# Sobel, attention and feed-forward tower: the carried edge rows of gy are written before the root's argument instead of after it

## What is computed

```python
kx, ky = _sobel_kernels()          # sy = [[1,2,1],[0,0,0],[-1,-2,-1]]
Ix = _dwconv(x, kx)
Iy = _dwconv(x, ky)
G = jnp.hypot(Ix, Iy)
return jnp.sum(G, axis=1)
...
h = jnp.concatenate([cls_tok, h], axis=1)
h = h + attention(layernorm(h))
h = h + ffn(layernorm(h))
```

## Time and profile before

| | |
|---|---|
| median of 3 runs | 1623.98 us (1623.11 to 1624.61) |
| the profiled execution | 1622.37 us, span 1620.3 us |
| VectorE busy | 1373.8 us, 85% of the span |
| PE busy | 839.6 us, 52% |
| ScalarE busy | 699.8 us, 43% |
| GpSimd busy | 110.1 us, 7% |
| DMA, mean | 35 GB/s |

### The profile page before, as it was taken

The page is one execution under the profiler, slowest core; times in us unless marked ns, Lnnn a source line. Parts: engine busy times, 40 slices in busy tenths (PEclk is TensorE's granted clock), DMA queues, the critical chain, the costliest instruction groups (busy, mean ns, idle before and its releaser), DMA issues.

```text
span 1620.3 us, 12694 instructions
## 1 busy us (share of the span) xinstructions
PE 839.6 (52%) x3318; PEld 655.5 (40%) x3318; DVE 1373.8 (85%) x2145; ACT 699.8 (43%) x1250; POOL 110.1 (7%) x154
## 2 busy tenths in 40 slices
PE   6663200466447743456537754256626764388543
PEld 3332100355336532344426543145525643376433
DVE  1999998899879999899879999899888999722676
ACT  1312332364375544164356553245446653132562
POOL 0000000001101000002101100002010100000000
PEclk9777655766569876667568976577568886577776
DMA  7000500013303510104302610104120300100001
GB/s 192 1 13 14 111 0 0 1 20 52 62 10 59 112 39 1 29 1 71 59 13 41 129 39 1 28 1 72 32 40 10 62 12 28 27 1 0 1 0 27
DMA packets 33421, 57.15 MB, mean 35 GB/s; under 512 B 6410, under 2 KB 23354, under 8 KB 31674
## 3 DMA queue, kind: packets, MB, share of 16 engines
q0 software_dynamic: 21024, 29.11, 11.1%
q1 hardware_dynamic: 12026, 26.31, 7.1%
q10 hardware_dynamic: 288, 0.79, 0.2%
HBM read 22.84 MB, written 4.25 MB: 17 GB/s over the span
## 4 chain that ended last, share of the span: by engine, by line
DVE 30%; issue 26%; ACT 15%; PE 12%; DMA 1%; DVEq 0%; ACTq 0%; SPq 0%
DVE arena L531 9%; DVE arena L528 6%; PE psum L1722 2%; ACT arena L1273 2%; DVE arena L872 2%; PE psum L1672 2%; PE psum L1694 1%; PE psum L1723 1%; PE psum L1576 1%; DVE red L544 1%; PE psum L1758 1%; ACT arena L1409 1%; ACT arena L1169 1%; DVE others L531 1%; ACT zT L1418 1%
## 5 line engine op out<-in xcount | busy, mean ns | idle before, releaser
L528 DVE TENSOR_TENSOR arena<-arena 128x768 f32<-128x768 f32 (+2 forms) x534 | 486.7, 967 | 45.8 <-ACT arena L1207 23.1
L531 DVE SCALAR_TENSOR_TENSOR arena<-arena 128x768 f32<-128x768 f32 (+2 forms) x224 | 201.4, 948 | 0.1
L1590 PE MATMUL psum<-zT,w1q 128*128 128x257 f32 x512 | 150.1, 431 | 41.8 <-ACT wout L1303 25.2
L1590 PEld LDWEIGHTS psum<-zT,w1q 128*128 128x128 f32 x512 | 111.3, 220 | 68.1 <-issue 27.5
L1576 PE MATMUL psum<-gpad,win 128*128 128x257 f32 x288 | 86.0, 442 | 54.9 <-ACT gpad L1285 54.9
L1238 ACT ACTIVATE arena<-arena 128x768 f32<-128x768 int16 x32 | 27.0, 843 | 175.6 <-DVE arena L531 175.2
L1694 PE MATMUL psum<-arena 128*128 128x257 f32 x128 | 50.6, 563 | 86.5 <-ACT arena L1392 65.3
L1576 PEld LDWEIGHTS psum<-gpad,win 128*128 128x128 f32 x288 | 62.6, 223 | 71.9 <-ACT gpad L1285 61.0
L531 DVE SCALAR_TENSOR_TENSOR arena<-img 128x768 f32<-128x768 f32 x88 | 79.5, 949 | 7.0 <-issue 6.4
L504 POOL DMA_DIRECT2D h<-others x60 | 51.7, 862 | 416.6 <-DVE others L531 347.7
L1169 ACT ACTIVATE arena<-arena 128x256 f32<-128x256 f32 x65 | 23.3, 409 | 118.4 <-DVE arena L531 68.2
(11 more groups left out here) (222 smaller groups left out, 1993.5 us busy)
## 6 DMA issues: line engine op xcount, KB each, us to landing
img<-x SPq DMA_DIRECT2D x36, 258.0 KB, 7.0
h<-others POOLq DMA_DIRECT2D x60, 128.0 KB, 2.7
arena<-nrows_mem POOLq DMA_DIRECT2D x18, 384.0 KB, 4.4
arena<-arena POOLq DMA_DIRECT2D x18, 384.0 KB, 4.1
arena<-img POOLq DMA_DIRECT2D x18, 384.0 KB, 4.9
out<-out SPq DMA_DIRECT2D x16, 256.0 KB
img<-x SPq DMA_DIRECT2D x48, 64.5 KB, 7.7
win<-w_in SPq DMA_DIRECT2D x4, 768.0 KB, 5.4
```

Of the source, the lines that this page charges most:

```text
L528: return v.tensor_tensor(o, a, b, op)
L531: return v.scalar_tensor_tensor(out=o, in0=a, scalar=s, in1=b, op0=op0, op1=op1)
L1590: ins = mm((A0, A1, B0, B1)[i % 4][:, 0:S], w1q[:, k, t * P:(t + 1) * P], zT[:, k, b, :], start=(k == 0), stop=(k == DT - 1))
```

## The change

The two writes of the next pair's edge rows move on VectorE from slot 5 to slot 4, ahead of whatever stands there, and each gets a wait for `hisq`, since it overwrites the q that ScalarE squares. They are then issued ahead of the root's argument, and no longer between the argument and the root. On ScalarE the negated copies of these rows move from behind slot 6 to behind slot 5: ahead of the square of the f16 value (line 1249), and no longer ahead of the next one (line 1254). There are 9 pairs with the edge rows (pairs 0 to 2 of three groups) and 6 with the negated copies (pairs 0 and 1). No instruction of an engine is added.

```diff
@@ magnitude_rows, VectorE
                 def with_carry(k):
-                    if k == 5 and i < PAIRS - 1:
+                    if k == 4 and i < PAIRS - 1:
                         for f in F:
+                            dve.wait_ge(hisq, n2 + f + 1)
                             edge_row(tmp[f][1], 2 * i + f + 4).then_inc(carried, 1)
                     slot(k)
@@ magnitude_rows, ScalarE
                     if k == 3 and i < PAIRS - 1:
                         for f in F:
                             s.activation(nrows[:, f], img[:, :, 2 * i + f + 2, 2:2 + W], ACT.Copy, scale=-1.0).then_inc(neg_rows, 1)
-                    if k == 6 and i < PAIRS - 2:
+                    if k == 5 and i < PAIRS - 2:
                         for f in F:
                             act.wait_ge(carried, g * (2 * (PAIRS - 1)) - 2 * (PAIRS - 1 - i) + f + 1)
                             s.activation(edge[:, (2 * i + f) % 4], tmp[f][1], ACT.Copy, scale=-1.0).then_inc(neg_edges, 1)
```

## The result

| | before | changed |
|---|---|---|
| median | 1623.55 us (1622.18 to 1625.36, 6 runs) | 1630.32 us (1629.46 to 1632.18, 6 runs) |
| ratio | | 1.0041, 95% interval 1.0029 to 1.0053 |
| span of the profiled execution | 1620.3 us | 1627.5 us |

The changed kernel is slower by 6.8 us, 0.41%. The forecast was 8.3 us slower, with a range that holds the measured time.

A forecast was written before the change was run, and what follows sets the result against it. The prediction took VectorE, busy 85% of the span, as the bound. Pairs 0, 1 and 2 add 0.89 + 1.74 + 0.14 = 2.77 us per group, 8.3 us over three, giving 1632.3 us against a 1623.98 median; range 1629.0 to 1635.0.

The forecast's parts named there:

- The quotient's square is no wait to fill: At the edge rows' new place on VectorE, the squares are long done; added waits cost 0 us in all nine pairs.
- Pair 2, 0.14: Between argument and f16 value and on to the correction, cover is lost: 0.14 us slower per group.
- Pair 1, 1.74: Argument, root, weights' copies and weighted values all start later, lengthening VectorE's wait: 1.74 us slower per group.
- Pair 0, 0.89: Late exponentials, then negated copies, delay ScalarE's square and VectorE's correction: 0.89 us slower per group.
- The earlier transfers give nothing: GpSimd's transfers for the next pairs start sooner, but nobody waits for their landing: gain 0.
- None of the losses is taken back later: Work behind pair 1 hangs on VectorE's result through each engine, so it all moves and no loss is recovered.
- swallowed shift in pair 1: Rival, chance 0.06: the 5.64 us wait absorbs the 1.74 us, leaving 3.1 us slower, 1627.1 us.
- transfers on the path: Rival, chance 0.03: VectorE's wait behind line 1207 is for gy's landing, so 5.2 us faster, 1618.8 us.
- dearer pair 0: Rival, chance 0.06: pair 0 costs all of its 1.74 us, 2.6 us more in total, 1634.9 us.
- tail: Rival, chance 0.03: a 1.28 us pause follows each table load in pair 0, 3.8 us more, 1636.1 us.

The follow-up runs named there:

- e3: The changed kernel with pair 1's edge rows back at slot 5 on VectorE; 1627.06 us, ratio to before 1.0015.
- e1: The changed kernel with ScalarE's negated copies back behind slot 6, so VectorE's part of the change alone; 1628.47 us, ratio to before 1.003.
- e6: The kernel before with ScalarE's copies of batch 3's transposed weights in pair 1 moved to slot 4, ahead of the root; 1613.62 us, ratio 0.9938.
- e2: The kernel before with ScalarE's negated copies moved behind slot 5, so ScalarE's part of the change alone; 1624.89 us, ratio 1.0003.
- e7: The kernel before with `own_heads` and `context` of batch 3 one slot later in pair 1; 1607.29 us, ratio 0.9899.
- e8: The changed kernel with `own_heads` and `context` of batch 3 one slot later in pair 1; 1619.85 us, ratio to before 0.9979.
- e10: The kernel before with pair 2's edge rows at slot 7 instead of 5, so pair 3's transfers begin 10.8 us later; 1623.96 us, ratio 0.9999.
- e4: The changed kernel with ScalarE's copies of batch 3's transposed weights in pair 1 moved to slot 4, ahead of the root; 1622.77 us, ratio to before 0.9991.

## Why the prediction was right

Step by step, as the prediction put them:

- *The quotient's square is no wait to fill: 0.* Right: the edge rows start with no idle time before them (790.38 above), and no row of the waits names that square.
- *Pair 2, 0.14.* It measured 0.13 on average; e3 and e1 show it too.
- *Pair 1, 1.74.* It measured 1.74 in each group, and the wait for the weighted values grew to 7.24 us, where 5.64 + 1.74 - 0.12 makes 7.26. e3, which leaves this move out, takes exactly it away, and e6 shows the link on which it rests: the copies stand behind the root. In e6 the wait for the weighted values shrinks by 3.0 us when they do not.
- *Pair 0, 0.89.* It measured 0.78. The negated copies took 1.47 us from their start to the square's (729.88 to 731.35), not 1.58: the row of two copies shows their time to the end, and the next instruction starts 0.1 us before that end. The mechanism is the one given, and e1 and e2 show that under the wait for TensorE both halves of the change are needed for it. The sentence that the wait for TensorE does not move held for the first two groups; in the third that wait was gone in two of three profiles. The loss stayed 0.78 us against the kernel before only because its groups all had the wait; e7 and e8 put it at 2.28 where TensorE is early, and the prediction had no such case.
- *The earlier transfers give nothing.* Right, and e10 shows it by the stronger test.
- *None of the losses is taken back later.* This step failed in part. The 7.9 us of the pairs do reach the last group, but there 2.8 us come back, and 1.7 us are added on the way in attend. The prediction had no term for either; they nearly cancel, and the net error is the 1.1 us between 7.9 and 6.8. The other 0.4 us between 8.3 and 7.9 are nearly all pair 0. That the total came out so near is in part luck: with the 2.8 alone it would have been 5.1 us slower, with the 1.7 alone 9.6.

The rivals: no swallowed shift in pair 1, no transfers on the path, no dearer pair 0 in this comparison. No table load has a tail: in pair 0 of the changed kernel the load begins at 726.77, takes 1.28 us, and the exponential follows at 728.07.

The clock accounts for the two unforeseen stretches as far as the profile tells. In the last group TensorE works on the weighted values of the first batch. There are four groups of matmuls, with a product of another kind behind them. Before and changed, the start of the first group and of that product:

```profile
1437.84 0.95 PE L1722 MATMUL psum<-arena 128*128 128x64 f32 x4
...
1444.32 3.79 PE L1647 MATMUL psum<-xT,win 128*128 128x257 f32 x8
```
```profile
1447.52 0.55 PE L1723 MATMUL psum<-arena 128*128 128x64 f32 x4
...
1451.53 3.79 PE L1648 MATMUL psum<-xT,win 128*128 128x257 f32 x8
```

The same four matmuls take 0.95 us before and 0.55 in the changed kernel, and the whole stretch 6.48 us before and 4.01 changed: 2.5 of the 2.8 us. The granted clock of the stretches around them (before, then changed; us; busy time of PE, PEld, DVE, ACT and POOL; the clock as a share of full speed; DMA):

```profile
1437.00:1441.00 4.00, 4.00 (x15) 3.35 (x13) 1.40 (x2) 1.37 (x7) 0.00 (x0) 0.50 0.00 0
```
```profile
1447.00:1451.00 4.00, 4.00 (x26) 3.36 (x24) 1.40 (x2) 1.74 (x8) 0.00 (x0) 0.93 0.00 0
```

0.50 is 1.2 GHz; 0.93 is 2.4 GHz for most of the stretch. In attend it goes the other way. Its 18 matmuls of line 1758 (1759 in the changed kernel) take 0.63 us longer, in a group in which attend as a whole is 0.72 us longer:

```profile
815.41 5.92 PE L1758 MATMUL psum<-arena,onehotT 128*128 128x256 f32 x18 [5.99 <-DVE arena L531]
```
```profile
821.20 6.55 PE L1759 MATMUL psum<-arena,onehotT 128*128 128x256 f32 x18 [5.99 <-DVE arena L531]
```

The granted clock over their second half was 0.87 before and is 0.74 in the changed kernel:

```profile
818.00:822.00 4.00, 3.34 (x13) 2.46 (x12) 2.62 (x5) 2.97 (x14) 1.24 (x3) 0.87 0.29 42
```
```profile
824.00:828.00 4.00, 3.74 (x13) 2.76 (x11) 2.04 (x5) 2.60 (x12) 1.03 (x3) 0.74 0.35 51
```

The other runs fit this: where attend is 15.65 us long (e3, first group) the same place shows a clock of 0.95, where it is 17.18 (e3, second group) 0.57, where it is 17.42 (e8, second group) 0.54. What TensorE's work before a stretch has to be for the one or the other is open. e1 and e8 have the short last group as well (102.09 and 102.23 us), e3 and e4 have the long one (104.67 and 104.92); e1 and e3 come to it equally late, so lateness alone does not decide it. No run was made that changes only this.

## What to carry to other kernels

Before work is moved into a wait, look whether the trace shows the wait: here the cover was needed between argument and root, and the place to which the rows went had 4.3 us of room and nothing to fill. Count what stands in the other engine's queue behind the instruction that becomes late; most of this loss went through three small copies for TensorE that happened to be queued behind the root. Do not count a wait for another engine as fixed cover: in pair 0 TensorE's lateness hid 1.5 of the 2.3 us that the move costs there, and in some groups of some runs it was not late. The long wait that the change lengthened was the thing worth working on: the kernel before with `own_heads` and `context` of batch 3 one slot later takes 1607.29 us and beats both; joined with e6's edit it was not tried.

## What the hardware showed that was not expected

The last group's attention, in which VectorE waits for TensorE, repeats between profiles of one kernel (104.71 to 104.78 us before, 101.86 to 102.02 changed, in three profiles each) and steps by 2.8 us between two kernels whose instructions there are the same. Such repetition is not sure: in pair 0 of the changed kernel's third group the weighted values took 4.14, 4.11 and 6.48 us in the three profiles, and it did not show in the pair's length only because ScalarE's square ended last there. An edit elsewhere can move them (the changed kernel, e1 and e8 have the short last group; the kernel before and the other six variants the long one), so a measured ratio of a few tenths of a per cent holds such steps beside the effect of the edit. Here it was -2.8 us in one place and +1.7 us in three others, against 7.9 us in the pairs.
